# A graph network on one core: edge scatters moved from behind the second attention layer into both attention sums

## The reference, cut to what matters

```
x = x + gatv2(layernorm(x), edges)          # two layers: 4 heads, then 1 head
x = x + slices(layernorm(x))                # softmax(x W) per head, pooled and spread back
x = x + relational(layernorm(x), edges, types)
x = x + experts(layernorm(x), second_edges) # the first that needs the second graph
...
# one attention layer:
m = xl[src] + xr[dst];  logits = (leaky_relu(m) * att).sum(-1)
ex = exp(logits - max over dst);  alpha = ex / sum over dst
out = segment_sum(alpha * xl[src], dst)     # the "attention sum"
```

## Time and profile before

| what | value |
|---|---|
| median of 3 runs | 9938.87 us (9934.84 to 9940.5) |
| span of the profiled execution | 9945.0 us, 0.06% above the median (no other time of that execution is given) |
| busy: PE, DVE, POOL, ACT | 5420.6 (55%), 4738.5 (48%), 4913.5 (49%), 1672.6 us (17%) |
| indirect DMAs into `tab_n` | 512, median 0.96 us of POOL each |
| gathers from `xl_g` | 1320, mean 0.97 us of POOL each |
| first attention sum, first gather to last | 1847.4 to 2188.1 us |
| second attention sum, first gather to last | 3037.5 to 3369.1 us |
| 392 scatters beside the slices' stage | 3409.4 to 3932.5 us |

### The profile page before, as it was taken

How to read it: one execution, slowest core, us unless ns; L and a number is a source line. 1 busy time by engine, 2 the same in 40 slices (tenths; PEclk the granted TensorE clock), 3 DMA queues, 4 the chain that set the end, 5 groups by cost and what they waited for, 6 DMA issues and landing times. The chain is left out here.

```text
span 9945.0 us, 91158 instructions
## 1 busy us (share of the span) xinstructions
PE 5420.6 (55%) x27074; PEld 3661.6 (37%) x27074; DVE 4738.5 (48%) x10464; ACT 1672.6 (17%) x4934; POOL 4913.5 (49%) x4961
## 2 busy tenths in 40 slices
PE   3227677556775411774456651444333747756496
PEld 3116455344554301443333331223222423334364
DVE  4227567785677601423421139445335344569422
ACT  1103211462111101210001111101000112236110
POOL 3660366655666576026646640564763336647012
PEclk7556788797888755887667775666666555569698
DMA  1101355343554300133323321444444223336211
GB/s 51 29 19 59 106 158 159 115 140 101 159 157 144 98 7 1 37 124 92 93 72 85 89 61 53 133 139 121 134 138 107 73 68 107 109 96 181 98 31 59
DMA packets 521088, 945.13 MB, mean 95 GB/s; under 512 B 144238, under 2 KB 306501, under 8 KB 520237
## 3 DMA queue, kind: packets, MB, share of 16 engines
q0 software_dynamic: 224784, 526.26, 19.3%
q1 hardware_dynamic: 295837, 413.04, 13.0%
HBM read 760.05 MB, written 178.24 MB: 94 GB/s over the span
## 5 line engine op out<-in xcount | busy, mean ns | idle before, releaser
L167 PE MATMUL ps<-g,oh 128*128 128x256 bf16 (+3 forms) x6160 | 1495.5, 400 | 1506.7 <-issue 654.0
L171 POOL DMA_INDIRECT g<-xl_g,xsrc x1320 | 1279.4, 969 | 1014.1 <-issue 365.7
L167 PEld LDWEIGHTS ps<-g,oh 128*128 128x128 f32 (+1 forms) x6160 | 1039.8, 176 | 1962.5 <-issue 1037.0
L171 POOL DMA_INDIRECT g<-gcn,xsrc x880 | 873.0, 992 | 839.1 <-SPq L127 453.8
L1227 DVE TENSOR_TENSOR h<-h,ps 128x256 f32 x1320 | 555.8, 421 | 1147.2 <-remote 699.8
L171 POOL DMA_INDIRECT g<-hx_rel,xtyp x440 | 431.5, 981 | 642.2 <-DVEq L124 451.7
L178 POOL DMA_INDIRECT tab_n<-n_pay,n_addr x512 | 553.1, 1080 | 352.2 <-issue 157.4
L167 PE MATMUL ps<-g,ident 128*128 128x256 f32 x1760 | 561.3, 446 | 250.7 <-issue 237.8
L171 POOL DMA_INDIRECT wide<-gat_rows,xs x536 | 506.9, 946 | 366.9 <-issue 155.4
L167 PE MATMUL ps<-w,hT 128*128 (+2 forms) x1808 | 508.1, 429 | 169.9 <-ACT hT L2616 148.1
L178 POOL DMA_INDIRECT tab_m<-m_pay,m_addr x416 | 418.2, 1005 | 312.3 <-DVE m_addr L627 188.2
(11 more groups left out here) (567 smaller groups left out, 9847.3 us busy)
## 6 DMA issues: line engine op xcount, KB each, us to landing
kept_g<-g SPq DMA_DIRECT2D x220, 256.0 KB
g<-kept_g SPq DMA_DIRECT2D x220, 256.0 KB
rowb<-dst_rows_m SPq DMA_DIRECT2D x81, 512.0 KB
kept_h<-gk SPq DMA_DIRECT2D x110, 264.0 KB
g<-kept_h SPq DMA_DIRECT2D x110, 264.0 KB
hx_rel<-tb SPq DMA_DIRECT2D x200, 128.0 KB
g<-xl_g,xsrc POOLq DMA_INDIRECT x1320
rowb<-dst_rows_n SPq DMA_DIRECT2D x33, 512.0 KB
```

What stands on the lines that cost most here:

```text
L167: return k.nc.tensor.matmul(out, lhsT, rhs, start=start, stop=stop, skip_group_check=True)
L171: return k.nc.gpsimd.indirect_dma_start(out=out, out_offset=None, in_=table, in_offset=bass.IndirectOffsetOnAxis(ap=index, axis=0), oob_is ...
```

## The change

Behind each pair of gathers in both attention sums one column of the second graph's edges is scattered: 110 in each sum. The batches ahead stay as they are, and `send_columns` at the head of the slices' stage issues what is left: 512 - 16 - 40 - 110 - 48 - 16 - 110 = 172 in place of 392.

```
-def seg_mean(k, T, table, dl, ex, out, H, kept, W=D, least=1.0e-30, M=None, own=None, x=None):
+def seg_mean(k, T, table, dl, ex, out, H, kept, W=D, least=1.0e-30, M=None, own=None, x=None, between=0):
...
                 for t in range(S * i, S * i + 2):
                     gather(k, g[:, t % (R * S), 0:W], table, k.xsrc[:, t:t + 1],
                            3200).then_inc(gathered[i % R].sem, gathered[i % R].up())
+                if between:
+                    send_columns(k, k.second, k.n_sent, between)
...
-def gat_layer(k, name, xT, Wl, Wr, att, bias, brow, H, acc, x=None, lists=None, sent=(0, 0)):
+def gat_layer(k, name, xT, Wl, Wr, att, bias, brow, H, acc, x=None, lists=None, sent=(0, 0), between=0):
...
-        seg_mean(k, T, table, k.dlA, L[:, :], acc[:, :], H, kept, M=M[:, :], own=own[:, :, :], x=x)
+        seg_mean(k, T, table, k.dlA, L[:, :], acc[:, :], H, kept, M=M[:, :], own=own[:, :, :], x=x,
+                 between=between)
...
-                  lists=finish_main, sent=(40, 48))
+                  lists=finish_main, sent=(40, 48), between=1)
...
-                  a['L0_gnn_att2'].rearrange("h c -> (h c)"), a['L0_gnn_b2'], brow, 1, h, x, sent=(16, 0))
+                  a['L0_gnn_att2'].rearrange("h c -> (h c)"), a['L0_gnn_b2'], brow, 1, h, x, sent=(16, 0), between=1)
```

## The result

| | time, median (us) | lowest to highest | span of the profiled execution |
|---|---|---|---|
| before | 9939.78 (20 runs) | 9926.45 to 9958.55 | 9945.0 |
| after | 9960.02 (20 runs) | 9944.84 to 9969.09 | 9956.5 |

The ratio is 1.0016 with a 95% interval of 1.001 to 1.0022: the change costs 0.16%, inside the 0.2% that was called no change, and 34 us over the predicted 9926. Two amounts of nearly 300 us cancel, as forecast, and the balance came out on the other side.

What follows compares the result with a forecast made beforehand. VectorE was taken as busiest in the sums, POOL's stream as starving the slices' stage. Removing scatters there, -287.2 us, plus 274.6 us added in POOL-bound sums gave -12.6 us: 9926 us, range 9840 to 9990.

Steps and rivals of the forecast that it cites:

- the 0.2% that was called no change: Whole kernel: 0.2% (20 us) is about what a measurement can tell from none; chance of landing within it 0.35.
- The mechanism it named: Slices' stage: POOL's stream of indirect transfers, 0.30 us apart, starves the other engines; nine blocks took 326.1 us beside scatters.
- The gain, 287.2 us: Slices' stage: with 172 scatters left, block 0 to 9 takes 38.9 us in place of 326.1.
- blocks 0 to 9 at 4.32 us once the stream has ended: Slices' stage: from block 0's sum on, full pace at once, 9 x 4.32 = 38.9 us.
- the lower bound of 267 us: Slices' stage: smallest gain, if block 0 came as late after the stream's new end as block 9 after the old, 26 us.
- The cost, 274.6 us: Both attention sums: POOL becomes the bound with three transfers a group, adding 134.5 and 142.6 us, less 2.5.
- price of 1.44 us for each transfer: Both attention sums: POOL time per transfer, mean of five POOL-bound stages; 330 transfers make 475.2 us a sum.
- The 2.5 us taken off for the two last scatters: Ends of both sums: the last scatter has no gather behind it, so 2 x 1.26 us was subtracted.
- -12.6: Whole kernel: gain and cost together, -287.2 + 274.6 us, applied to the median of 9938.87 us.
- The break-even price of 1.459: Both sums: microseconds per transfer at which the change in time is nothing; 1.429 gives minus 20 us, 1.489 plus 20.
- Rival B: Both sums: scatters hide better, 1.26 to 1.40 us per transfer; 9807 us at 1.26, 9854 at 1.33; chance 0.20.
- That the gain in the slices' stage fails: Slices' stage: would need another cause for the standstill than the stream; given no chance of its own.

Runs made afterwards that it cites:

- group 1: Chip with kernel before at 9992.8 us; ratios against it: first sum only 1.0009, every second group 0.9994, gathers for scatters 1.0009, rest after every 8th scatter 0.9941.
- groups 1 and 5: Rests in the kernel before, nothing moved: after every 8th scatter 9928.48 us, 0.9941, on one chip; after every 2nd 9768.37 us, 0.9776, on the other.
- The kernel with gathers: Changed kernel with each of the 220 moved scatters replaced by a gather into a spare buffer: 10002.05 us, 1.0009 against the kernel before.
- group 3: Another chip: kernel before 8306.33 us, changed kernel 8549.23 us (1.0294); with rests after every 2nd scatter, kernel before 1.0290, changed kernel 1.0294.
- groups 2, 4 and 6: Three chips with kernel before at 8304.2, 8314.6 and 8304.2 us; kernel before or changed kernel with rests between scatters: ratios 1.0144 to 1.0301.
- group 5: Kernel before, nothing moved, POOL waiting for landing after every 2nd of the 392 scatters: 9768.37 us against 9993.22 us, ratio 0.9776.

## Why the prediction was wrong

**The mechanism it named is there, on the chips that have it.** A stream of transfers on POOL stops the other engines, rests end that (0.9776 with nothing else changed), and on such a chip moving scatters exchanges one full cost for another. The first measurement and group 1 show the exchange, groups 1 and 5 the rests. But the forecast had a sign, and that came from two terms of nearly 300 us, each missed by 3%.

**The gain, 287.2 us, was 277.9.** The first failed step is "blocks 0 to 9 at 4.32 us once the stream has ended". The blocks start at full pace 23 us after the last scatter, not at once. The same 26 us stood in the earlier trace rows and were the basis of the lower bound of 267 us; I set them aside, as the engines had come through to block 0 inside the stream. That one block says nothing about the next. The kernel with gathers has it again: block 0 within the first 8 us after the stream, block 1 24 us after it.

**The cost, 274.6 us, was 283.1** at the first scatter of the stage. The second sum's price of 1.44 us for each transfer was right (1.441; +142.9 us against 142.6). The first sum's was too low: 1.479, 12.7 us above 134.5 (147.2). That is the second failed step: 1.44 us was taken for both sums. It took more in all than the second from the start. The longer transfers are hardly the reason, as the kernel with gathers shows. Which property of the first sum is (ScalarE, for one, has 52 us of work in 100 there and 4 in the second) stays open. The 2.5 us taken off for the two last scatters were not saved in the sums either, and 7 us came back outside them: 12.7 + 0.3 + 2.5 - 7.0 = 8.5 us too low in all. The rate of 69 transfers in 100 us and the pauses of 2 to 3 us were as written.

**The balance.** 283.1 - 277.9 = 5.3 us at block 24 in place of -12.6. Either error alone would have left the sum just below zero (-3.3 or -4.1 us); the two together turned it. To this come 6 us in stages that the change does not touch, whose cause isn't known. The medians differ by 20.2 us, and their interval allows 10 to 22; the profiled spans differ by 11.5 us, since the profiled execution before lay some 6 us above its median and the one after 2 us below. The break-even price of 1.459 was that of an uncertain gain: with 277.9 it is 1.445, and the mean price was 1.460. An error of 1% in the price was enough to lose the forecast's sign, so the sum carried no more than "about nothing".

**Rival B** (no starving beside a stream: 1.26 to 1.40 us for each) was judged by one chip's trace. Four other chips are in its case: 1.351 and 1.276 us for each in the changed sums (group 3; in groups 2, 4 and 6 the changed sums are within 2 us of these). But then the gain of the slices' stage is gone as well, and the result is not B's 9807 but a loss of 2.9%. B kept the standstill in one stage and took it away in the other; it should have been priced with both ends, and as the rival on the slower side. "That the gain in the slices' stage fails" got no chance of its own, because the standstill ended with the stream in the earlier trace rows. That argument holds for a chip, not for the kernel: on the chip of group 3 the shorter list gave back nothing (t2 505.8 and 506.0 us) in place of 287 us. That the time lay near the predicted 9926 us at all rests on the kind of chip that was met first.

The Trainium skill's rule (Runtime: NRT & Kernel Launch, "Instruction fetch mechanics", that the fetching of code ahead is mostly hidden) would have no engine run dry beside POOL's stream. The chips of groups 2, 3, 4 and 6 agree with that (t1 144.6 us in group 3). The first measurement doesn't (614.0 us), nor do the chips of groups 1 and 5, by the sorting's 1733 to 1772 matmuls in place of 5150. That fetching is what stops there was not shown: the trace names no wait for it, only "issue" or a late DMA.

## What to carry to other kernels

Before work is moved away from a queue because others stand still beside it, try a short rest in that queue: here a wait for landing after every 2nd transfer gave 2.2% on such a chip (one chip, four executions), and moving the work gave nothing. On a chip without the standstill the same wait costs 2.9%, so find out first which kind is at hand. Where the queue is what is full, a moved transfer costs nearly the time that it occupies there (1.13 us each in group 3, of 1.26), and moving it away pays only if something waits for the queue at the old place; there POOL idled 285 us instead. And where one trace shows engines that stop with nothing to wait for, take a trace on a second chip before a gain is built on it.

## What the runs showed of the hardware

- The kernel before took 9940 to 9993 us in the first measurement and on the chips of groups 1 and 5, and 8303 to 8315 us on the four of groups 2, 3, 4 and 6 (the executions of one group within 0.4%), with single transfers of the same length (a gather of the layers takes 0.946 us in the median in both). The difference lies in how other engines fare beside POOL's indirect transfers: 1772 or 5150 matmuls in the same 600 us. All kernels of a group fell on the same side. What makes a chip one or the other was not found, nor whether it lasts: each was met once.
- On the first kind, a rest of 1.1 us more in 3.6 us ended the standstill (t1 142.9 us), one in 11.3 us left most of it (487.6 us), none gave 614.0 us (group 5, group 1 and the first measurement; the three were not run on one chip).
- Such a rest, a wait until the transfer has landed, costs POOL 1.1 us: 1.41 us in place of 0.30 us between two transfers (groups 1 and 5). On the second kind of chip it costs 1.4% (every 4th) and 2.9% (every 2nd) of the kernel's time, so no version here beats the kernel before on both.
